# A fused layer norm, dilated attention and FFN kernel: the output product is issued ahead of the next segment's first two hidden products

## The chip, the cores and the metric

The kernel runs on one core of a Trainium2 chip. The metric is the device time of one execution in microseconds (us); lower is better. TensorE does matrix products into PSUM, ScalarE, VectorE and GpSimd work on tiles beside it, and the SyncE queue (SPq in the rows) issues the transfers. Each engine works through its own instructions in the order in which the kernel writes them, and semaphores tie the engines together.

## The reference

```python
x = L0_attn_x                                  # (16, 1024, 256), float32
xn = _layernorm(x, axis=-1)
x = x + _L0_attn_ref(xn, Wqkv, Wout) + _L0_ffn_ref(xn, W1, b1, W2, b2)

# attention: 16 heads of 16, segments of 512 tokens, every 8th token a key
scores = jnp.einsum('bhspd,bhskd->bhspk', q4, k4)          # 512 x 64 a head
scores = scores.reshape(B, H, S, nb, BLOCK_M, Kn)
c = jnp.max(scores, axis=4, keepdims=True)
w = jnp.exp(scores - c)
den = jnp.sum(w, axis=-1) + 1e-10
num = jnp.einsum('bhsnmk,bhskd->bhsnmd', w, v4)
out = num / den[..., None]                                  # then times Wout
# FFN, inner width 1024
h = jax.nn.relu(jnp.einsum('bsh,hi->bsi', hidden_states, W1) + b1)
return jnp.einsum('bsi,ih->bsh', h, W2) + b2
```

## The kernel before

The 16 x 1024 tokens are 32 segments of 512. One `step(s, ...)` handles three segments at once, each engine with a `step` of its own: the FFN and the attention's output of segment `s`, the scores, exponentials and weighted values of segment `s + 1`, and the layer norm, keys and queries of segment `s + 2`; GpSimd and VectorE prepare the statistics of `s + 3`. `first_step` and `lead_step` fill this pipeline (`s` = -2 and -1), steps 0 and 1 are written out, steps 2 to 27 run in a loop of two steps a turn, and steps 28 to 31 are written out again. The order of the work is the order of the code; no scheduler moves anything.

Every product is done in three matmuls, each operand being split into a high and a low part (`xt_hi`, `xt_lo`; `w_hi`, `w_lo`): `three_products`, line 994. The matmuls are 128 x 128 by 128 x 512. A segment's FFN has eight hidden tiles `i`: `first_product` (6 matmuls) fills `h_bank[i % 2]`, ScalarE's `hidden` makes `h_hi` (L603) and `h_full` (L605) of it, GpSimd's `hidden_lo` the difference `h_lo` (L524), and `second_product` (6 matmuls) adds tile `i` to the two y_banks. The first two hidden tiles of the next segment are made at the end of a step (`tail_tiles`); tile 2 needs the bank of tile 0 back (`h_ready`).

The attention's way through a step's end: `queries` (12 matmuls), which ScalarE casts to `q_hi` (L646); behind them on ScalarE `attention_hi` (L616, `att_hi`), and on GpSimd `attention_out` (L531) and `attention_lo` (L536, `att_lo`), the low part of the normalised attention of segment `s`. `output_product` (12 matmuls) multiplies both parts by Wout and adds them to the y_banks, which VectorE then transposes (L941). It begins with

```python
pe.wait_ge(att_hi, (s + 1) * QUADS)
pe.wait_ge(att_lo, (s + 1) * QUADS)
```

`weighted_values` (L1159) writes numerators and sums of segment `s + 1` into two pairs of banks, misc and s_banks. ScalarE's `attention_drain` copies each pair to `num_den` (L623): the first releases misc, the second s_banks, and the next step's first `scores` (L1063) wait for both, and for the packed keys `k_pack`. Both copies also release the transfer of the sums on the SyncE queue (`den_to_dram`, L381), from which VectorE makes the inverse denominators (`invert_den`, L833).

GpSimd's `inverse_deviation` (L514, L516) makes `rstd` of segment `s + 3` for the layer norm.

Of the kernel before, what the change touches and what calls it, by code (L numbers as in the profile page):

```python
# [48 lines left out]
def ln_attention_ffn(nc, x, wq_t, wkv_t, wout_t, w1, b1, w2, b2, out):  # L49
# [19 lines left out]
    with ExitStack() as ctx:  # L69
# [220 lines left out]
        def tail_tiles(s, attention):  # L290

            if isinstance(s, int) and s < 0:
                return 0, [(0, 1), (EARLY, EARLY + 1)][s + 2]
            return s + 1, (0, 1) if attention else ()
# [205 lines left out]
        def _(pool):  # L500
# [7 lines left out]
            def inverse_deviation(s, par):  # L508

                pool.wait_ge(stats_ready, s + 1)  # L510
                pool.wait_ge(xn_ready, past(s))
                pool.wait_ge(consts_made, 3)
                w = tiles(par)
                pool.tensor_tensor(var_eps[:, 0:w], mean_var[:, 0:w, 1], eps[:, 0:w], ALU.add).then_inc(var_ready, 1)  # L514
                pool.wait_ge(var_ready, s + 1)
                pool.tensor_tensor(rstd[:, 0:w], var_eps[:, 0:w], minus_half[:, 0:w],  # L516
                                   ALU.pow).then_inc(rstd_ready, 1)
# [15 lines left out]
            def attention_lo(s, quad, par):  # L533
                pool.wait_ge(att_ready, s * QUADS + quad + 1)
                pool.wait_ge(att_hi, s * QUADS + quad + 1)
                pool.tensor_tensor(att_part[1][:, quad], att[:, quad], f32(att_part[0][:, quad]),  # L536
                                   ALU.subtract).then_inc(att_lo, 1)
# [9 lines left out]
            def step(s, par, ffn, attention, norm, load):  # L547
                first, _ = tile_steps(s, ffn)
                for i in range(LAG, NH):
                    if i in first:  # L550
                        hidden_lo(past(s), first[i])
                    if i == 2 and ffn and later(s):
                        residual(s - 1, 1 - par)
                    if i == 5 and by_rows(s):
                        residual(s, par)
                if attention and ffn:
                    for quad in range(QUADS):
                        attention_out(s, quad)
                    for quad in range(QUADS):
                        attention_lo(s, quad, par)  # L560
                segment, tail = tail_tiles(s, attention)
                for i in tail:
                    hidden_lo(segment, i)
                if load:
                    inverse_deviation(s + 3, 1 - par)

            def first_step():
                inverse_deviation(0, 0)
# [22 lines left out]
        def _(act):  # L591
# [26 lines left out]
            def attention_drain(s, quad):  # L618

                n = (s + 1) * QUADS + quad + 1  # L620
                act.wait_ge(pv_psum, n)
                act.wait_ge(att_ready, past(n - QUADS))
                act.copy(num_den[:, quad], pv_banks[quad][:]).then_inc(num_den_ready, 1)  # L623
# [66 lines left out]
            def step(s, par, ffn, attention, norm, load):  # L690
                first, _ = tile_steps(s, ffn)
                for i in range(LAG, NH - 1):
                    if i == 3 and norm and par == 0:
                        keys_hi(s)
                    if attention:
                        exponential(s, i - LAG)
                    if i in first:
                        hidden(past(s), first[i])
                if ffn and not attention:
                    for quad in range(QUADS):  # L700
                        attention_hi(s, quad, par)
                if norm:
                    transposed_hi(s, par)
                if NH - 1 in first:
                    hidden(s, NH - 1)
                if attention:
                    exponential(s, PAIRS - 3)
                if attention:
                    exponential(s, PAIRS - 2)
                if norm:  # L710


                    pair_keys_hi(s, par)
                if attention:
                    exponential(s, PAIRS - 1)
                if norm:
                    for m in range(DH):
                        queries_hi(s, m)
                if attention and ffn:
                    for quad in range(QUADS):  # L720
                        attention_hi(s, quad, par)
                if attention:
                    attention_drain(s, 0)
                segment, tail = tail_tiles(s, attention)
                for i in tail:
                    hidden(segment, i)
                if attention:
                    attention_drain(s, 1)

            iterations(act, first_step, lead_step, step)  # L730

# [257 lines left out]
        def _(pe):  # L989
# [173 lines left out]
            def step(s, par, ffn, attention, norm, load):  # L1163
                first, second = tile_steps(s, ffn)
                if attention:
                    scores(s, 0)
                    scores(s, 1)
                for i in range(LAG, NH):
                    if i == 3 and norm and par == 0:
                        transpose_keys(s)  # L1170
                    if i == 5 and norm and par == 0:
                        keys_values(s)
                    if i == 6 and norm and par == 0:
                        transpose_k(s)
                    if i == NH - 1 and norm and by_tensor(s):
                        transpose_x(s, par)
                    if i in first:
                        first_product(past(s), first[i], par if ffn else 1 - par)
                    if attention and i > LAG:
                        scores(s, i - 1)  # L1180
                    if i in second:
                        second_product(past(s), second[i])
                if ffn:
                    second_product(s, NH - 2)
                if attention:
                    scores(s, NH - 1)
                if norm:
                    for m in range(DH):
                        queries(s, par, m)
                if ffn:  # L1190
                    second_product(s, NH - 1, (0,))
                if attention:
                    weighted_values_waits(s, par, norm)
                if ffn:
                    second_product(s, NH - 1, (1,))
                if attention:
                    weighted_values(s, 0, par)
                    weighted_values(s, 1, par)
                segment, tail = tail_tiles(s, attention)
                for i in tail:  # L1200
                    first_product(segment, i, 1 - par if attention else par, norm)
                if ffn:
                    output_product(s, par)

            pe.wait_ge(consts_made, 3)
            pe.wait_ge(masks_made, 2)
# [60 lines left out]
```

## Time and profile before

| | us |
|---|---|
| time, median of 3 runs | 1082.38 (1081.92 to 1085.41) |
| the profiled execution's own time | 1080.21 |
| its span in the trace | 1078.4 |
| TensorE busy | 1047.4 (97%) |
| VectorE busy | 818.8 (76%) |
| ScalarE busy | 647.9 (60%) |
| GpSimd busy | 622.7 (58%) |

Busy is the time in which an engine has an instruction in work, and all engines run side by side. The mean granted clock of TensorE is 0.997 of full speed. The ends of matmuls are modelled: a row of 0.39 us overlaps the next, and the distance between two starts is the pace.

### The profile page before, as it was taken

The page shows a single profiled execution, that of the slowest core. Times are in us where ns is not written, and L with a number is a line of the kernel's source. Part 1 is how long each engine was busy: PE and PEld are TensorE (multiplying, and loading weights), DVE is VectorE, ACT ScalarE, POOL GpSimd, SP SyncE. Part 2 cuts the span into 40 slices and gives each one's busy share as a digit, 9 for nine tenths or more (in the row PEclk, how much of TensorE's full clock was granted, in tenths as well). Part 3 has the DMA queues.
Part 4 walks back from the last instruction along what each step waited for, and adds up shares of the span by engine and source line. Part 5 has one row for each costly group of instructions (what it writes and reads, how often), then busy time and mean ns, then how long its engine had stood idle before and what let it go on. Part 6 is the DMA issues. An engine that isn't in the chain of part 4 may idle for free.

```text
span 1078.4 us, 19171 instructions
## 1 busy us (share of the span) xinstructions
PE 1047.4 (97%) x5381; PEld 813.1 (75%) x5381; DVE 818.8 (76%) x1464; ACT 647.9 (60%) x1080; POOL 622.7 (58%) x487
## 2 busy tenths in 40 slices
PE   5899999999999999999999999999999999999996
PEld 4577787777787777787777787777787777777775
DVE  7787877877877877877877777877877877878632
ACT  5656665666666566665656656566665666655651
POOL 5255565656565665565655655665565656556562
PEclk9999999999999999999999999999999999999999
DMA  5357777787877777777687887777777787866733
GB/s 190 97 154 206 221 210 212 191 233 197 234 223 192 199 214 219 225 213 209 185 234 197 231 224 191 197 215 219 221 209 217 186 229 199 242 192 182 192 108 117
DMA packets 153287, 216.37 MB, mean 201 GB/s; under 512 B 27312, under 2 KB 96432, under 8 KB 153264
## 3 DMA queue, kind: packets, MB, share of 16 engines
q1 hardware_dynamic: 153264, 216.09, 72.3%
q8 instruction: 12, 0.20, 0.1%
q14 instruction: 11, 0.09, 0.0%
HBM read 100.41 MB, written 58.46 MB: 147 GB/s over the span
## 4 chain that ended last, share of the span: by engine, by line
PE 86%; DMA 6%; DVE 3%; SPq 3%; issue 2%; ACT 1%; POOL 0%; POOLq 0%; DVEq 0%; ACTq 0%
PE h_bank L994 36%; PE y_bank L994 36%; PE s_banks L1063 5%; PE misc L1159 3%; PE s_banks L1159 2%; PE misc L994 2%; DMA k_dram<-k_lo 2%; DMA yt_dram<-y_mem 1%; SPq L399 1%; DVE xn L805 1%; DMA xt_dram<-z 1%; DMA k_pack<-k_dram 1%; SPq L438 1%; DVE s_max L822 0%; SPq L421 0%
## 5 line engine op out<-in xcount | busy, mean ns | idle before, releaser
L524 POOL TENSOR_TENSOR h_lo<-h_full,h_hi 128x512 fp32r<-128x512 f32 x256 | 335.8, 1312 | 394.0 <-ACT h_full L605 384.0
L611 ACT ACTIVATE w_exp<-w_exp 128x512 f32<-128x512 f32 x256 | 161.5, 632 | 245.8 <-DVE w_exp L828 243.9
L603 ACT ACTIVATE h_hi<-h_bank,b_cols 128x512 fp32r<-128x512 f32 x256 | 174.5, 682 | 71.2 <-PE h_bank L994 63.9
L994 PE MATMUL h_bank<-xt_hi,w_hi 128*128 128x512 f32 x512 | 206.9, 404 | 0.0
L994 PE MATMUL h_bank<-xt_lo,w_hi 128*128 128x512 f32 x512 | 200.7, 392 | 0.0
L994 PE MATMUL h_bank<-xt_hi,w_lo 128*128 128x512 f32 x512 | 200.2, 391 | 0.0
L994 PE MATMUL y_bank<-h_hi,w_hi 128*128 128x512 f32 x496 | 194.9, 393 | 1.6 <-ACT w_exp L611 1.6
L822 DVE TENSOR_REDUCE s_max<-s_banks 128x8 f32<-128x512 f32 x254 | 170.9, 673 | 33.2 <-PE s_banks L1063 33.0
L994 PE MATMUL y_bank<-h_lo,w_hi 128*128 128x512 f32 x496 | 194.0, 391 | 0.0
L994 PE MATMUL y_bank<-h_hi,w_lo 128*128 128x512 f32 x496 | 193.7, 391 | 0.0
L828 DVE TENSOR_TENSOR w_exp<-s_banks,s_max 128x512 f32<-128x512 f32 x254 | 175.7, 692 | 11.0
L605 ACT ACTIVATE h_full<-h_bank,b_cols 128x512 f32<-128x512 f32 x256 | 174.4, 681 | 0.0
L994 PEld LDWEIGHTS h_bank<-xt_hi,w_hi 128*128 128x128 f32 x512 | 96.2, 188 | 47.2 <-issue 27.1
L994 PEld LDWEIGHTS h_bank<-xt_hi,w_lo 128*128 128x128 f32 x512 | 96.4, 188 | 21.0
L994 PEld LDWEIGHTS y_bank<-h_hi,w_hi 128*128 128x128 f32 x496 | 93.6, 189 | 22.2 <-issue 2.0
L994 PEld LDWEIGHTS h_bank<-xt_lo,w_hi 128*128 128x128 f32 x512 | 96.6, 189 | 17.9
L994 PEld LDWEIGHTS y_bank<-h_lo,w_hi 128*128 128x128 f32 x496 | 93.7, 189 | 20.5
L994 PEld LDWEIGHTS y_bank<-h_hi,w_lo 128*128 128x128 f32 x496 | 93.2, 188 | 20.6
L941 DVE STREAM_TRANSPOSE y_mem<-y_bank 128x512 f32<-128x512 f32 x62 | 44.4, 717 | 77.8 <-PE y_bank L994 77.8
L1063 PE MATMUL s_banks<-q_pack,k_pack 96*128 96x512 f32 x248 | 95.2, 404 | 3.3 <-DMA k_pack<-k_dram 1.6
L536 POOL TENSOR_TENSOR att_lo<-att,att_hi 128x512 fp32r<-128x512 f32 x62 | 78.7, 1290 | 23.8 <-ACT att_hi L616 23.7
L531 POOL TENSOR_TENSOR att<-num_den,rden_rows 128x512 f32<-128x512 f32 x62 | 84.3, 1382 | 5.3 <-DMA rden_rows<-rden_dram 4.8
(135 smaller groups left out, 1513.5 us busy)
## 6 DMA issues: line engine op xcount, KB each, us to landing
q_pack<-q_hi SPq DMA_DIRECT2D x248, 128.0 KB, 2.5
x_raw<-x SPq DMA_DIRECT2D x32, 512.0 KB, 4.8
rden_rows<-rden_dram SPq DMA_DIRECT2D x128, 128.0 KB, 4.6
x_b<-x SPq DMA_DIRECT2D x32, 512.0 KB, 4.5
q_pack<-q_lo SPq DMA_DIRECT2D x124, 128.0 KB, 2.4
yt_dram<-y_mem SPq DMA_DIRECT2D x124, 128.0 KB, 3.6
y_mem<-yt_dram SPq DMA_DIRECT2D x31, 512.0 KB, 4.6
out<-x_b SPq DMA_DIRECT2D x31, 512.0 KB, 3.1
```

The lines of the kernel that those rows point to most:

```text
L524: pool.tensor_tensor(h_part[1][:, i % HBUF], h_full[:, i % HBUF], f32(h_part[0][:, i % HBUF]), ALU.subtract).then_inc(h_lo, 1)
L531: pool.tensor_tensor(att[:, quad], num_den[:, quad, 0], rden_rows[:, quad], ALU.mult).then_inc(att_ready, 1)
L536: pool.tensor_tensor(att_part[1][:, quad], att[:, quad], f32(att_part[0][:, quad]), ALU.subtract).then_inc(att_lo, 1)
L603: act.activation(h_part[0][:, i % HBUF], h_bank[i % 2][:], ACT.Relu, bias=b1_cols[:, i:i + 1]).then_inc(h_hi, 1)
L605: act.activation(h_full[:, i % HBUF], h_bank[i % 2][:], ACT.Relu, bias=b1_cols[:, i:i + 1]).then_inc(h_ready, 1)
L611: act.activation(w_exp[:, pair], w_exp[:, pair], ACT.Exp).then_inc(w_ready, 1)
L822: dve.tensor_reduce(s_max[:, pair], ps.rearrange("p t n i -> p n t i"), AX.XY, ALU.max).then_inc(max_ready, 1)
L828: dve.tensor_tensor(w_exp[:, pair].rearrange("p (t n i) -> p t n i", t=T, n=NB), ps, top, ALU.subtract).then_inc(s_shifted, 1)
L941: dve.transpose(y_blocks[:, :, a].rearrange("p i t n -> p t i n"), y_bank[a][:].rearrange("p (t i n) -> p t i n", t=T, n=PW)).then_inc(y_r ...
L994: mm = pe.matmul(ps, stationary[a], moving[b], start=start and c == 0 and n == 0, stop=stop and c == len(pairs) - 1 and n == 2, skip_group ...
L1063: pe.matmul(s_bank[n % 2], k_pack[0:PR, pair % (PAIRS // 2), pair // (PAIRS // 2)], q_pack[0:PR, pair], start=True, stop=True).then_inc(s_ ...
L1159: mm = pe.matmul(pv_banks[quad][PW * j:PW * (j + 1), a], v[rows, 1 - par, pair], w_exp[rows, pair], start=True, stop=True)
```

## The change

Three pieces of code trade places, each inside the same step and on its own engine; no instruction is added or removed. TensorE issues `output_product` of segment `s` straight behind the weighted values, and the next segment's first two hidden products behind it. ScalarE makes the second copy of the sums straight behind the first, ahead of the two hidden tiles. GpSimd makes the inverse deviations ahead of its two `h_lo`.

```diff
--- before.py
+++ after.py
@@ -558,11 +558,11 @@
                         attention_out(s, quad)
                     for quad in range(QUADS):
                         attention_lo(s, quad, par)
+                if load:
+                    inverse_deviation(s + 3, 1 - par)
                 segment, tail = tail_tiles(s, attention)
                 for i in tail:
                     hidden_lo(segment, i)
-                if load:
-                    inverse_deviation(s + 3, 1 - par)
 
             def first_step():
                 inverse_deviation(0, 0)
@@ -721,11 +721,11 @@
                         attention_hi(s, quad, par)
                 if attention:
                     attention_drain(s, 0)
+                if attention:
+                    attention_drain(s, 1)
                 segment, tail = tail_tiles(s, attention)
                 for i in tail:
                     hidden(segment, i)
-                if attention:
-                    attention_drain(s, 1)
 
             iterations(act, first_step, lead_step, step)
 
@@ -1196,11 +1196,11 @@
                 if attention:
                     weighted_values(s, 0, par)
                     weighted_values(s, 1, par)
+                if ffn:
+                    output_product(s, par)
                 segment, tail = tail_tiles(s, attention)
                 for i in tail:
                     first_product(segment, i, 1 - par if attention else par, norm)
-                if ffn:
-                    output_product(s, par)
 
             pe.wait_ge(consts_made, 3)
             pe.wait_ge(masks_made, 2)
```

TensorE, at the end of an even step in the loop, before. The rows are instructions with their waits; the first two are the weighted values, `h_bank` the first products of tiles 0 and 1, `y_bank<-att` the output product.

```order
L1159 MATMUL misc<-w_exp,v 32x512 x8
L1159 MATMUL s_banks<-w_exp,v 32x512 x8
L1005 REGISTER_ALU
L994 MATMUL h_bank0<-xt_hi,w1_hi 128x512 [waits q_lo]
L994 MATMUL h_bank0<-xt_lo,w1_hi 128x512
...
L994 MATMUL h_bank1<-xt_hi,w1_hi 128x512 [waits q_lo]
...
L994 MATMUL y_bank0<-att_hi,wout_hi 128x512 [waits att_lo,att_hi]
L994 MATMUL y_bank0<-att_lo,wout_hi 128x512
...
L1062 REGISTER_ALU [waits k_packed,num_den_ready,pair_packed0]
```

The same place after the change.

```order
L1159 MATMUL misc<-w_exp,v 32x512 x8
L1159 MATMUL s_banks<-w_exp,v 32x512 x8
L994 MATMUL y_bank0<-att_hi,wout_hi 128x512 [waits att_lo,att_hi]
L994 MATMUL y_bank0<-att_lo,wout_hi 128x512
...
L994 MATMUL h_bank0<-xt_hi,w1_hi 128x512 [waits q_lo]
L994 MATMUL h_bank0<-xt_lo,w1_hi 128x512
...
L994 MATMUL h_bank1<-xt_hi,w1_hi 128x512 [waits q_lo]
...
L1062 REGISTER_ALU [waits k_packed,num_den_ready,pair_packed0]
L1063 MATMUL s_banks<-q_pack,k_pack 128x512 [waits s_shifted] x2
L994 MATMUL h_bank0<-xt_hi,w1_hi 128x512 [waits h_ready]
```

The instruction that waits for `att_lo` and `att_hi` now stands directly behind the weighted values, and twelve first products stand between it and the scores.

ScalarE, the end of the same step, as a difference: the two copies to `num_den` and the hidden tiles.

```order
 L623 COPY num_den<-misc 128x1024 [waits att_ready]
+L621 REGISTER_ALU
+L623 COPY num_den<-s_banks 128x1024 [waits att_ready,pv_psum]
 L601 REGISTER_ALU [waits h_psum]
 L603 ACTIVATE h_hi<-h_bank0,b1_cols 128x512 [waits h_used,h_lo]
...
 L603 ACTIVATE h_hi<-h_bank1,b1_cols 128x512 [waits h_used,h_lo]
 L605 ACTIVATE h_full<-h_bank1,b1_cols 128x512
-L621 REGISTER_ALU
-L623 COPY num_den<-s_banks 128x1024 [waits att_ready,pv_psum]
```

The copy of `s_banks` moved from behind the two tiles to ahead of them.

## Rows read from the trace of the kernel before

**Rows 1.** The page, TensorE's busy time in us, share, instructions.

```profile
PE 1047.4 (97%) x5381; PEld 813.1 (75%) x5381; DVE 818.8 (76%) x1464; ACT 647.9 (60%) x1080; POOL 622.7 (58%) x487
```

**Rows 2.** TensorE's waits: us in total, times, longest us.

```profile
PE y_bank L994 <- POOL h_lo L524: 7.2, 2, 5.2
...
PE s_banks L1063 <- DMA k_pack<-k_dram: 1.6, 3, 1.0
```

**Rows 3.** Timeline of TensorE, segment 14's step: start us, us, instruction.

```profile
516.36 0.39 PE L994 MATMUL h_bank<-xt_hi,wq_lo 128*128 128x512 f32 x1
...
519.92 0.50 PE L994 MATMUL h_bank<-xt_hi,w_hi 128*128 128x512 f32 x1
...
522.77 0.39 PE L994 MATMUL y_bank<-att_hi,wout_hi 128*128 128x512 f32 x1
...
525.49 0.70 PE L1063 MATMUL s_banks<-q_pack,k_pack 96*128 96x512 f32 x2
...
527.41 0.39 PE L994 MATMUL y_bank<-h_hi,w_hi 128*128 128x512 f32 x1
```

**Rows 4.** Timelines of ScalarE, GpSimd and VectorE, the same step.

```profile
516.79 0.59 ACT L646 CAST q_hi<-h_bank 128x512 fp32r<-128x512 f32 x1
517.27 1.14 ACT L616 CAST att_hi<-att 128x512 fp32r<-128x512 f32 x2
519.31 1.01 ACT L623 COPY num_den<-misc 128x1024 f32<-128x1024 f32 x1 [0.90 <-PE misc L1159]
...
522.33 0.68 ACT L605 ACTIVATE h_full<-h_bank,b_cols 128x512 f32<-128x512 f32 x1
...
524.25 1.02 ACT L623 COPY num_den<-s_banks 128x1024 f32<-128x1024 f32 x1
...
518.03 2.53 POOL L536 TENSOR_TENSOR att_lo<-att,att_hi 128x512 fp32r<-128x512 f32 x2 [0.75 <-ACT att_hi L616]
523.16 2.65 POOL L524 TENSOR_TENSOR h_lo<-h_full,h_hi 128x512 fp32r<-128x512 f32 x2 [2.59 <-ACT h_full L605]
...
526.05 1.02 POOL L516 TENSOR_TENSOR rstd<-var_eps,minus_half 128x4 f32<-128x4 f32 x1
...
520.93 0.38 DVE L760 BATCH_NORM_AGGREGATE mean_var<-stats 128x2 f32<-128x6 f32 x4
```

**Rows 5.** Timelines of GpSimd and TensorE, last segment.

```profile
1063.54 1.71 POOL L524 TENSOR_TENSOR h_lo<-h_full,h_hi 128x512 fp32r<-128x512 f32 x1
...
1065.39 0.55 PE L994 MATMUL y_bank<-w_hi,h_hi 128*128 128x256 f32 x1 [5.17 <-POOL h_lo L524]
```

**Rows 6.** Timelines of GpSimd and TensorE, steps of segments 0 and 29.

```profile
64.84 2.54 POOL L536 TENSOR_TENSOR att_lo<-att,att_hi 128x512 fp32r<-128x512 f32 x2 [3.73 <-ACT att_hi L616]
...
66.17 0.50 PE L994 MATMUL h_bank<-xt_hi,w_hi 128*128 128x512 f32 x1
...
1005.53 2.53 POOL L536 TENSOR_TENSOR att_lo<-att,att_hi 128x512 fp32r<-128x512 f32 x2 [0.52 <-ACT att_hi L616]
...
1007.15 0.50 PE L994 MATMUL h_bank<-xt_hi,w_hi 128*128 128x512 f32 x1
```

**Rows 7.** Timeline of ScalarE, segment 30's step.

```profile
1036.90 1.01 ACT L623 COPY num_den<-misc 128x1024 f32<-128x1024 f32 x1 [1.17 <-PE misc L1159]
...
1041.81 1.02 ACT L623 COPY num_den<-s_banks 128x1024 f32<-128x1024 f32 x1
```

**Rows 8.** The chain that ended last: start us, us, what held it.

```profile
1043.48 1.88 DMA den_dram<-num_den
...
1070.30 4.56 PE y_bank L994 x36
```

**Rows 9.** Windows: stretch, length, busy us (count) by engine, granted clock, DMA share, GB/s.

```profile
44.00:48.00 4.00, 0.84 (x4) 0.58 (x5) 3.53 (x5) 0.84 (x2) 1.19 (x1) 1.00 0.83 204
48.00:51.40 3.40, 3.40 (x10) 2.62 (x9) 3.33 (x9) 1.01 (x3) 0.00 (x0) 0.50 0.82 178
...
104.00:108.00 4.00, 3.25 (x14) 2.69 (x15) 2.36 (x5) 0.14 (x1) 1.66 (x3) 1.00 0.69 146
```

## The prediction

> **What bounds the kernel now.** I began with the busy shares: TensorE is busy for 97% of the span [rows 1]. Next I read what TensorE itself waits for [rows 2]. Its waits on GpSimd sum to 7.2 us in two places, both in the last segment, and its waits on the packed keys to 1.6 us in three places. Nothing else of the 32 segments' steady work shows in that list, so TensorE is the bound and has almost no idle time that an order could give back. A change of order can then do three things: open a hole in TensorE's row, close one of the few that exist, or move the two ends of the program.
>
> Then I read one step of the loop around the change, first on TensorE [rows 3]. The last query product starts at 516.36, behind the weighted values the first product of the next segment's tile 0 at 519.92, the output product at 522.77, and the next step's scores at 525.49. Each block of 12 matmuls takes 2.72 us (522.77 to 525.49), that is 0.227 us a matmul; the first block takes 2.85 because its first weight load is not hidden.
>
> The other engines' rows of the same step [rows 4] give what the output product needs. ScalarE casts the second half of the queries from 516.79 (the last query matmul ends at 516.36 + 0.39 = 516.75), then casts att_hi from 517.27. GpSimd starts att_lo at 518.03, behind the first of these casts, and makes both quads in 2.53 us: it is done at **520.56**. So att_lo comes 3.8 us behind TensorE's own last query matmul, whatever else the step does. Before, the output product starts 2.2 us later than that, and never waits.
>
> **The output product, moved ahead of the two first products.** It now wants to start where the first product started, at 519.92. It waits for both quads of att_lo, which end 0.64 us later. From GpSimd's end to TensorE's start I take the one place that shows it, in the last segment [rows 5]: h_lo ends at 1063.54 + 1.71 = 1065.25, the matmul starts at 1065.39, so 0.14. The output product starts at 520.70, and the stall is 520.70 - 519.92 = **0.78 us** a step. TensorE's sequence is fixed, so all that is queued behind the waiting matmul (12 output matmuls, 12 first products, the scores) moves by this much; nothing fills the hole. The weight load that is exposed behind a wait was exposed at this place before too, so it adds nothing.
>
> Does the stall stay in every step? The step shown is segment 14's. Its two rows, att_lo's end and the start of the matmul behind the weighted values, stand 0.64 to 0.66 us apart in each of the 28 steps from segment 1 to 28, since both hang on TensorE's query products; 28 x 0.78 = 21.8. Two steps lie outside that pattern [rows 6]: segment 0, att_lo ends 67.38 against 66.17, stall 1.21 + 0.14 = 1.35; segment 29, 1008.06 against 1007.15, 0.91 + 0.14 = 1.05. Segment 30 is part of the end, below. Together **24.2 us**.
>
> **The first products, 2.72 us later.** Tile 0's chain is now closer to its users. In the step shown its first matmul starts at 519.92, ScalarE's h_full ends at 523.01 and GpSimd's h_lo starts at 523.16 [rows 3, 4]. Less the 0.1 us of exposed load that the new place does not have, h_full ends 2.99 and h_lo of tile 0 about 3.14 + 1.3 = 4.44 us behind the first matmul. TensorE needs h_full after 12 matmuls (2.72) and two scores, and h_lo after six matmuls more. Scores and six matmuls take 527.41 - 525.49 = 1.92, of it the six 1.38, so the needs come at 3.26 and 4.64. With 0.14 for the signal they are there at 3.13 and 4.58. Both just fit, by 0.13 and 0.06, where before they had seconds. A weight load cannot then run far ahead, so a little may show: at least nothing, at most 0.15 us at each of two places (an exposed load costs 0.1). I take 0.05 us a step over 30 steps, **1.5 us**; the bounds are 0 and 9.
>
> **The copy of the second sums ahead of the tiles (ScalarE).** In the step shown it moves from 524.25 to right behind the first copy, 519.31 + 1.01 = 520.3 [rows 4]. ScalarE is idle there until tile 0 arrives, and that now arrives later, so it costs nothing. Before, it ended at 525.27, 0.22 us ahead of the scores that wait for it: just in time, and hidden. So in the loop the earlier copy gives nothing. It lets the queue send the denominators some 1.5 us earlier, in the shadow of 97% TensorE; no gain.
>
> **The inverse deviations ahead of the tiles (GpSimd).** Their statistics end at 520.93 + 0.38 = 521.31 [rows 4], and they take 0.2 and 1.02 us (the second is the rstd row), in a stretch where GpSimd now waits for tile 0's h_full until 520.70 + 2.82 + 2.99 = 526.5. Hidden. If that cover were gone, 1.2 us would fall on h_lo and, at a slack of 0.06, nearly all on TensorE; the statistics would have to be 4 us later for that.
>
> **Waits that the stall absorbs.** TensorE's three waits for the packed keys, 1.03 at the most, 1.6 in all [rows 2], stand at the scores. The keys' chain hangs on the query products, so a TensorE that arrives 0.8 us later waits for 0.25 at one place and not at the other two: **-1.3 us**.
>
> **The end.** Here the copy does pay. In segment 30's step no later work hides it: the chain that ended last runs from this copy of the sums over the denominators' transfer to the last matmuls at 1070.30 [rows 8]. In that step the first copy starts at 1036.90 and the second at 1041.81 [rows 7]. Behind the first it would start at about 1036.90 + 0.96 = 1037.86: 3.95 us earlier. TensorE's row near the end has 5.17 us of waiting [rows 5], more than those 3.95 plus the step's own stall (1.35 in the worst step above), so the whole chain moves up and segment 30's stall disappears in it: **-3.95 us**.
>
> **Sum.** 24.2 + 1.5 - 1.3 - 3.95 = +20.4 us. The profiled execution took 1080.21 us (span 1078.4 and 1.8 around it), which gives 1100.6. The median shown is 2.2 us above that execution, which gives 1102.8. Between the two I predict **1102**.
>
> **Rivals.**
> (a) *No stall, only the end's gain.* The output product finds att_lo ready, and the end's 3.95 us (with up to 1.5 lost at tile 0) makes it 1082.4 - 3.95 = **1078 to 1080, faster**. It decides at 0.78 us: ScalarE's casts or GpSimd's two subtractions would have to end that much earlier against the query products. Against it: the change moves nothing that stands ahead of them on either engine, and the distance is constant over 28 steps. For it: only the inferred ends of matmuls and of GpSimd's instructions, which this reading trusts to some tenths. 8%.
> (b) *Part of the stall, about 3.95 / 28 = 0.14 us a step*, so that loss and gain cancel, within 0.3% of 1082: 3%.
> (c) *A second stall behind the first.* Tile 0's chain, with 0.06 us of slack, misses by more than the signal's time, for example because the wait is held in TensorE's instruction queue ahead of the matmul and the next loads start cold: 0.2 to 0.4 us more a step, x 30 = 6 to 12 us on top, **1107 to 1113**. 9%.
> (d) *The clock.* Behind 44 to 48 us, in which TensorE was busy for 0.84 us, the stretch from 48 to 51.4 has a granted clock of 0.50, the lower level of 1.2 GHz [rows 9]; at half the pace it loses 1.7 us. If each stall did that, 30 x 1.7 = 51 us would come on top, **1153**. Against it: the stretch from 104 to 108 us, which holds the wait of 1.03 us for the keys, longer than the stall foreseen, has a granted clock of 1.00 [rows 9]. 2%. The Trainium skill speaks for this rival: "TensorE: Matmul & The Clock Gate", section "A second HAM failure mode: psum-queue depth-cycling", says that frequent short idle times between groups of matmuls can make the clock swing between its two levels. By that rule the time would be (d)'s; the trace, with one such wait and no fall, does not bear it out, though it shows none that recurs.
>
> **How the numbers follow.** My forecast of one stall a step holds 78%. Its own range is 1096 (the exposed load behind the wait hidden, 28 x 0.1 less, no cost at tile 0, and the profiled run's base) to 1107. The 80% range adds part of (c), at its bound of 9 us at tile 0: **1096 to 1110**. What measures as no change here is 0.3%, about 3 us. Faster by more is (a), 8%; within it (b), 3%; slower everything else, 89%.
>
> **What the new profile would show.** TensorE idle 0.6 to 0.8 us before y_bank<-att_hi in every step, released by GpSimd's att_lo, some 20 us in the list of waits in 28 to 31 places. The second num_den copy right behind the first, and the rstd rows ahead of the h_lo rows. Nearly no wait for k_pack. Step pairs of the loop longer by 1.6 us. From the second copy of the last attention step to the end, the same 36 to 37 us as before. The prediction is wrong if the output product starts within 0.2 us of the weighted values' end; if the waits stand at h_bank or y_bank<-h_hi instead (c); if the granted clock leaves 1.0 inside the loop (d); or if the end does not come 4 us closer to segment 30's weighted values.

## The result, and the profile after

| | before | after |
|---|---|---|
| median, us | 1082.15 (1081.91 to 1085.41, 4 runs) | 1101.86 (1099.53 to 1104.19, 4 runs) |
| profiled execution, us | 1080.21 | 1099.53 |
| span, us | 1078.4 | 1097.7 |

The change makes the kernel slower: ratio 1.018, 95% interval [1.015, 1.0209]. The forecast was 1102, range 1096 to 1110.

The first lines of the page after, with the span and the busy times. TensorE has 4.3 us more of busy time than in [rows 1], though it does the same matmuls; the span has 19.3 us more. So most of the loss must be waiting.

```profile
span 1097.7 us, 19171 instructions
PE 1051.7 (96%) x5381; PEld 813.3 (74%) x5381; DVE 819.5 (75%) x1464; ACT 653.1 (59%) x1080; POOL 640.0 (58%) x487
```

TensorE's waits after (us in total, times, longest). Against [rows 2] one group is new, 30 waits on att_lo; h_lo is down from 7.2 us in two places to 3.2 in one; the row for k_pack is gone. The 1.2 us put down to "issue" is the output product of segment 0.

```profile
PE y_bank L994 <- POOL att_lo L536: 21.6, 30, 0.9
...
PE y_bank L994 <- POOL h_lo L524: 3.2, 1, 3.2
...
PE y_bank L994 <- issue: 1.2, 1, 1.2
```

TensorE's timeline of the same step as in [rows 3] (segment 14's). The output product starts at 532.11, 1.78 us behind the row of the weighted values, where a start without a wait came at 1.00 (518.92 to 519.92 before). The difference is the stall: 0.78. The last two rows show a second, small effect: h_bank's last matmul to the first y_bank is 0.31 instead of 0.23, and the next distance is 0.33.

```profile
530.33 1.06 PE L1159 MATMUL s_banks<-w_exp,v 64*32 64x512 f32 x16
532.11 0.47 PE L994 MATMUL y_bank<-att_hi,wout_hi 128*128 128x512 f32 x1 [0.72 <-POOL att_lo L536]
...
534.95 0.39 PE L994 MATMUL h_bank<-xt_hi,w_hi 128*128 128x512 f32 x1
...
537.67 0.63 PE L1063 MATMUL s_banks<-q_pack,k_pack 96*128 96x512 f32 x2
...
539.29 0.39 PE L994 MATMUL h_bank<-xt_hi,w_lo 128*128 128x512 f32 x1
539.60 0.49 PE L994 MATMUL y_bank<-h_hi,w_hi 128*128 128x512 f32 x1
539.93 0.40 PE L994 MATMUL y_bank<-h_lo,w_hi 128*128 128x512 f32 x1
```

ScalarE and GpSimd in that step, the answer to [rows 4]. att_lo ends at 529.44 + 2.53 = 531.97, and TensorE starts 0.14 later. The two copies stand side by side; the rstd rows stand ahead of h_lo, in idle time.

```profile
530.71 1.01 ACT L623 COPY num_den<-misc 128x1024 f32<-128x1024 f32 x1 [0.90 <-PE misc L1159]
531.62 1.02 ACT L623 COPY num_den<-s_banks 128x1024 f32<-128x1024 f32 x1
...
529.44 2.53 POOL L536 TENSOR_TENSOR att_lo<-att,att_hi 128x512 fp32r<-128x512 f32 x2 [0.74 <-ACT att_hi L616]
...
533.43 1.34 POOL L516 TENSOR_TENSOR rstd<-var_eps,minus_half 128x4 f32<-128x4 f32 x1
538.07 2.66 POOL L524 TENSOR_TENSOR h_lo<-h_full,h_hi 128x512 fp32r<-128x512 f32 x2 [3.30 <-ACT h_full L605]
```

Where the 19.3 us of span lie, in us between starts of the weighted values' row on s_banks (each start read from the timelines). These stretches come back below for the experiments.

| | start to step 3 | 24 loop steps, 3 to 27 | steps 27 to 30 | step 30 to the end | span |
|---|---|---|---|---|---|
| before | 162.84 | 776.46 | 97.28 | 41.82 | 1078.4 |
| after | 163.89 | 797.44 | 97.54 | 38.83 | 1097.7 |
| difference | +1.05 | +20.98 | +0.26 | -2.99 | +19.3 |

The end. ScalarE's last two copies, in segment 30's step: the second now starts 0.91 us behind the first, where [rows 7] had 4.91.

```profile
1059.19 1.01 ACT L623 COPY num_den<-misc 128x1024 f32<-128x1024 f32 x1 [1.17 <-PE misc L1159]
1060.10 1.02 ACT L623 COPY num_den<-s_banks 128x1024 f32<-128x1024 f32 x1
```

The chain that ended last (start, us) still begins with that copy and ends in the same 36 matmuls. But these took 6.05 us, where [rows 8] have 4.56.

```profile
1061.77 1.88 DMA den_dram<-num_den
...
1088.13 6.05 PE y_bank L994 x36
```

The windows show the clock at that place. First after (columns: stretch, length, busy us and count for PE, PEld, DVE, ACT and POOL, granted clock, share of DMA, GB/s), then before:

```profile
1088.00:1091.00 3.00, 2.87 (x15) 2.90 (x16) 0.00 (x0) 0.00 (x0) 0.00 (x0) 0.60 0.02 5
1091.00:1095.00 4.00, 3.17 (x23) 2.96 (x21) 1.38 (x2) 0.00 (x0) 0.00 (x0) 0.87 0.15 56
```

```profile
1070.00:1076.00 6.00, 4.54 (x36) 4.37 (x36) 1.38 (x2) 0.00 (x0) 0.15 (x1) 1.00 0.13 46
```

After, the last product begins behind an idle time of 3.2 us and runs at a granted clock of 0.60, near the lower level of 1.2 GHz. Before, a low clock came too, but earlier, behind the wait of 5.17 us [rows 5], where TensorE had little to do (columns: stretch, length, PE busy, clock, share of DMA, GB/s):

```profile
1062.00:1066.00 4.00, 0.61 (x3) 0.89 0.01 4
1066.00:1070.00 4.00, 2.29 (x11) 0.68 0.33 131
```

### The profile page after: what moved, and what is told of

Same layout as the page of the kernel before. It is cut to its first block and busy times, and to the rows that moved or that the text cites. A ratio compares the mean times of both kernels' runs of the same rounds, so it can differ in the third digit from the quotient of the medians.

```text
span 1097.7 us, 19171 instructions
## 1 busy us (share of the span) xinstructions
PE 1051.7 (96%) x5381; PEld 813.3 (74%) x5381; DVE 819.5 (75%) x1464; ACT 653.1 (59%) x1080; POOL 640.0 (58%) x487
## 5 line engine op out<-in xcount | busy, mean ns | idle before, releaser
L822 DVE TENSOR_REDUCE s_max<-s_banks 128x8 f32<-128x512 f32 x254 | 171.8, 677 | 116.2 <-PE s_banks L1063 115.9
L994 PE MATMUL h_bank<-xt_hi,w_hi 128*128 128x512 f32 x512 | 203.1, 397 | 0.0
L994 PE MATMUL y_bank<-h_hi,w_hi 128*128 128x512 f32 x496 | 197.6, 398 | 1.6 <-ACT w_exp L611 1.6
L828 DVE TENSOR_TENSOR w_exp<-s_banks,s_max 128x512 f32<-128x512 f32 x254 | 175.6, 691 | 11.0
L994 PEld LDWEIGHTS h_bank<-xt_hi,w_lo 128*128 128x128 f32 x512 | 96.4, 188 | 20.4
L861 DVE TENSOR_TENSOR xt_lo<-xt_raw,xt_hi 128x512 fp32r<-128x512 f32 x58 | 37.5, 688 | 59.8 <-ACT xt_hi L642 59.8
```

The source lines that it names most:

```text
L822: dve.tensor_reduce(s_max[:, pair], ps.rearrange("p t n i -> p n t i"), AX.XY, ALU.max).then_inc(max_ready, 1)
L828: dve.tensor_tensor(w_exp[:, pair].rearrange("p (t n i) -> p t n i", t=T, n=NB), ps, top, ALU.subtract).then_inc(s_shifted, 1)
L861: dve.tensor_tensor(token_order(xt[1][:, par, c]), block_order(xt_raw[:, c]), token_order(f32(xt[0][:, par, c])), ALU.subtract).then_inc(x ...
L994: mm = pe.matmul(ps, stationary[a], moving[b], start=start and c == 0 and n == 0, stop=stop and c == len(pairs) - 1 and n == 2, skip_group ...
```

## The experiments

The theory to test was the prediction's: TensorE waits for att_lo, 0.78 us a step, and the other two parts matter at the end alone. The rival: the order as such costs time (tile 0's chain, the clock), so that a product placed elsewhere would not get the 20 us back. The comparisons with the kernel before were made on other chips than the result's, where its median was 1084.05 to 1085.10; each ratio is against runs on the same chip. 

**copy_only**: the kernel before with ScalarE's part alone.

```diff
                 if attention:
                     attention_drain(s, 0)
+                if attention:
+                    attention_drain(s, 1)
                 segment, tail = tail_tiles(s, attention)
                 for i in tail:
                     hidden(segment, i)
-                if attention:
-                    attention_drain(s, 1)
```

> The kernel before with only ScalarE's second copy of the sums moved ahead of the two hidden tiles. Theory A (in the loop the change costs what TensorE waits for att_lo, and the copy pays only at the end): nothing changes in the loop, the steps keep 64.56 us a pair; the end comes 3.95 us closer, of which up to 1.5 us may be lost to a lower granted clock in the last 36 matmuls: 1078.2 to 1079.7 us. Rival B (the copy is what costs in the loop, by holding up ScalarE ahead of tile 0): tile 0's h_hi starts later and the time is 1082 or more.

Measured: 1076.99 us (6 runs) against 1085.10, ratio 0.9932 [0.991, 0.9954]. That is more than the end alone. By the trace (span 1074.5) the stretches are -0.15, -1.69, -0.02 and -2.04 us against before's: part of the gain lies in the loop. Rows of SyncE's queue, the transfer of the sums and the keys of the following step, show what moved there; first before, then copy_only:

```profile
525.30 1.17 SPq L381 DMA_DIRECT2D den_dram<-num_den  x2
...
547.27 0.43 SPq L354 DMA_DIRECT2D k_dram<-k_hi  x1
...
553.12 1.28 SPq L364 DMA_DIRECT2D k_pack<-k_dram  x3
```

```profile
523.65 1.17 SPq L381 DMA_DIRECT2D den_dram<-num_den  x2
...
546.42 0.32 SPq L354 DMA_DIRECT2D k_dram<-k_hi  x1
...
551.50 1.44 SPq L364 DMA_DIRECT2D k_pack<-k_dram  x3
```

The queue waits at `den_to_dram` for the second copy; with the copy early it sends the sums, the keys and the packed keys 1.65, 0.85 and 1.62 us earlier (of which 0.1 to 0.15 is the whole step's earlier place). Why the packed keys gain more than the keys was not followed. TensorE's waits for the keys fall from 1.6 us [rows 2] to 0.6. The profiled executions lie 3.9 us apart and the medians 8.1: before's runs on that chip spread over 6.5 us, and before's trace is of a quick execution (1080.21 us). What such a quick one does not show of before stands under deviation_only.

**queue_late**: copy_only, but SyncE sends the sums no sooner than the next step's first scores are done. ScalarE's copy stays early, so that only the queue is late.

```diff
-            def den_to_dram(s):
+            def den_to_dram(s, held=False):
 
-                sp.wait_ge(num_den_ready, (s + 1) * QUADS)
+                if held:
+                    sp.wait_ge(s_psum, (s + 1) * PAIRS + 1)
+                else:
+                    sp.wait_ge(num_den_ready, (s + 1) * QUADS)
...
-                    den_to_dram(s + 1)
+                    den_to_dram(s + 1, norm)
```

> copy_only, but the SyncE queue sends the denominators of a segment only when the first scores of the next step are done, some 0.6 us later than in the kernel before (not in the last two steps, where the queue has nothing behind it). Theory Q (the early copy also helps in the loop, because the queue, held until 525.3 by the copy's end, runs 1.6 us late, and brings the packed keys late to the scores): the waits for k_pack come back, and of the 8 us that copy_only gained the 4 us of the loop are lost: 1080 to 1084 us on a chip where before takes 1082 to 1085. Rival E (all of the gain is at the end, the rest is chance between runs): as copy_only, 1076 to 1079 us.

Measured: 1086.74 us (12 runs) against 1084.05, ratio 1.0031 [1.0013, 1.0048], above the range of either theory but on theory Q's side. The gain in the loop is lost and more (24 steps in 782.85 us, copy_only 774.77, before 776.46), while the end keeps its part (38.79 us against before's 41.82). TensorE's list of waits names the keys ten times:

```profile
PE s_banks L1066 <- DMA k_pack<-k_dram: 6.5, 10, 1.3
```

So a late queue does cost time in the loop, through the packed keys: it is all that differs from copy_only. The experiment holds the queue longer than before did, so that it shows the way of the copy's effect and not its size.

**deviation_only**: the kernel before with GpSimd's part alone (`inverse_deviation` ahead of the two `hidden_lo`).

> The kernel before with only GpSimd's part. Theory A: no difference, within 0.3% of before; TensorE's waits for the packed keys and the one of 1.6 us behind the loop stay, since neither its code nor the SyncE queue moves. Rival C: 3 us or more away from before.

Measured: 1083.58 us (12 runs) against 1084.05, ratio 0.999 [0.997, 1.001]. Nothing in the time, in the order of before. Its profiled execution took 1084.15 us, near the medians of before on these chips, and its trace (span 1082.4) shows where a usual execution is slower than the quick one behind before's trace: +3.07, +0.40, -1.14 and +1.67 us in the four stretches. In the first, TensorE's wait for the keys ahead of the loop is 1.97 us instead of 1.03, and the clock falls behind it; in the last, the final product takes 5.99 us instead of 4.56, at the low clock, though the copy stands where before has it (columns as in the windows above, TensorE alone):

```profile
106.00:110.00 4.00, 3.76 (x10) 0.58 0.70 147
...
1072.00:1076.00 4.00, 3.18 (x15) 0.50 0.01 4
```

Against this trace copy_only's stretches are -3.22, -2.09, +1.12 and -3.71 us, together -7.9: the size of its gain in the medians. That such executions are the usual ones of before is an inference from their times; only one was traced.

**product_only**: the kernel before with TensorE's part alone (`output_product` ahead of the two `first_product`).

> The kernel before with only TensorE's part of the change: output product behind the weighted values, the first two products behind it. Theory A: besides the 0.78 us at att_lo, ScalarE's second copy of the sums now stands behind two tiles that come 3.5 us later, and the next scores wait for it: it would end about 28.75 us into a step in which TensorE is ready at 26.25 (counted as in the step shown, 520 added), so 2.7 us more a step, 80 us in all, and 3.4 us at the end: 1180 to 1195 us, with TensorE's waits at s_banks released by ScalarE's num_den. Rival B (the copy's place in the loop does not matter to TensorE): 1100 to 1106 us.

Measured: 1207.82 us (2 runs), ratio 1.1153 [1.1122, 1.1183]: slower than the expected 1180 to 1195 by another 13 to 28 us. The stall on att_lo is the same as in after; what is new stands at the next scores. TensorE's waits, then one of them:

```profile
PE s_banks L1063 <- issue: 42.3, 17, 2.5
PE s_banks L1063 <- ACT num_den L623: 32.0, 13, 2.5
PE y_bank L994 <- POOL att_lo L536: 21.4, 30, 0.7
```

```profile
623.57 0.72 PE L1063 MATMUL s_banks<-q_pack,k_pack 96*128 96x512 f32 x2 [2.47 <-ACT num_den L623]
```

The second copy, left behind both hidden tiles on ScalarE, comes as much later as the tiles do, and 30 scores wait up to 2.5 us each. 13 of the waits are put down to num_den by name; the other 17 end 0.1 to 0.2 us behind the same copy. The copy's move is part of what makes the product's move affordable.

What the expectation left out is the clock. Behind these waits it falls in some steps and stays in others: in 15 of the 30 steps matmuls behind the scores start 0.43 us apart instead of 0.23. Two places, each from the wait on; the first falls and the second does not:

```profile
513.00:519.00 6.00, 6.00 (x15) 0.50 0.58 143
...
550.40:556.00 5.60, 5.59 (x25) 1.00 0.48 116
```

The 24 loop steps take 877.6 us, twelve of the quickest pairs (71.56) would take 858.7: 19 us in the loop, the size of the excess. The mean granted clock is 0.969. This is the prediction's rival (d), at 2.5 us of waiting and not at 0.7.

**product_and_copy**: after without GpSimd's part, that is with `inverse_deviation` behind the two `hidden_lo` as before.

```diff
-                if load:
-                    inverse_deviation(s + 3, 1 - par)
                 segment, tail = tail_tiles(s, attention)
                 for i in tail:
                     hidden_lo(segment, i)
+                if load:
+                    inverse_deviation(s + 3, 1 - par)
```

> The changed kernel without GpSimd's part (the inverse deviations stay behind the two h_lo). Theory A: they are off the path in either place: the same as the changed kernel, 1099 to 1104 us. Rival C (they matter where tile 0 has no slack, through VectorE, which waits for rstd ahead of the scores' maxima): 3 us or more away from it.

Measured: 1170.7 us (4 runs), ratio 1.0813 [1.0791, 1.0836], 69 us above after. My own theory (A) falls, the rival that this part carries something holds. GpSimd's and VectorE's rows in one of the steps:

```profile
606.51 2.66 POOL L524 TENSOR_TENSOR h_lo<-h_full,h_hi 128x512 fp32r<-128x512 f32 x2 [6.10 <-ACT h_full L605]
...
609.40 1.18 POOL L516 TENSOR_TENSOR rstd<-var_eps,minus_half 128x5 f32<-128x5 f32 x1
```

```profile
610.85 0.41 DVE L772 TENSOR_SCALAR xn_keys<-x_keys,mean_var,rstd 128x256 f32<-128x256 f32 x1 [5.67 <-POOL rstd L516]
```

GpSimd stands idle for 6.1 us waiting for a hidden tile that the change made late, with the short rstd instructions queued behind it. VectorE waits 5.67 us for them, and behind `xn_keys` in its queue stand the softmax rows of the same step (L822, L828). TensorE then waits for these and for xn_keys:

```profile
PE s_banks L1063 <- DVE w_exp L828: 23.6, 16, 1.5
...
PE misc L1108 <- DVE xn_keys L772: 19.5, 15, 2.4
```

With 5.4 us for the keys these groups hold 45 us more of waiting than after's list, and TensorE's busy time is 19 us longer. What lengthens the busy time was not followed.

**dose**: after, with two more GpSimd subtractions of 128 x 128 ahead of each step's att_lo, whose results nobody uses. If att_lo's end sets TensorE's start, the stall grows by their duration.

```diff
...
+                if quad == 0:
+                    for half in range(2):
+                        pool.wait_ge(dose_made, past(s * 2 + half))
+                        pool.tensor_tensor(k_mask_t[:], att[:, quad, half * P:(half + 1) * P],
+                                           f32(att_part[0][:, quad, half * P:(half + 1) * P]),
+                                           ALU.subtract).then_inc(dose_made, 1)
                 pool.tensor_tensor(att_part[1][:, quad], att[:, quad], f32(att_part[0][:, quad]),
                                    ALU.subtract).then_inc(att_lo, 1)
```

> The changed kernel with more of the suspected wait: two further GpSimd subtractions of 128x128 ahead of att_lo in each step, their results not used. From the rows of before (0.2 us for 128x4, 1.27 for 128x512) I estimate 0.47 each, 0.94 us a step. Theory A: every us by which att_lo is later is a us of TensorE, 30 x 0.94 = 28 us more than the changed kernel, 1130 us (1120 to 1140); the exact number is 30 times the duration that its trace shows. Rival B: at most 5 us more, below 1107.

Measured: 1130.65 us (4 runs), ratio 1.042 [1.0391, 1.0449]. One step, GpSimd and then TensorE: two added instructions that put off att_lo's row by 0.96 us (577.88 to 578.84), and a wait of 1.66 instead of 0.72, that is +0.94. Over 30 steps that makes 28 us; after itself was not timed on this chip, but its median of 1101.86 and the 1100.62 of changed_again, below, lie 29 and 30 us lower.

```profile
577.88 1.01 POOL L540 TENSOR_TENSOR k_mask_t<-att,att_hi 128x128 f32<-128x128 f32 x2 [0.73 <-POOL att L532]
578.84 2.51 POOL L543 TENSOR_TENSOR att_lo<-att,att_hi 128x512 fp32r<-128x512 f32 x2
```

```profile
581.50 0.47 PE L1001 MATMUL y_bank<-att_hi,wout_hi 128*128 128x512 f32 x1 [1.66 <-POOL att_lo L543]
```

The clock, in windows with TensorE alone (stretch, length, busy, granted clock, share of DMA, GB/s). The step just shown keeps 1.00; segment 0's, with its wait of 2.1 us at 67 to 70, does not.

```profile
67.00:70.00 3.00, 1.24 (x4) 0.85 0.84 205
70.00:73.00 3.00, 3.00 (x10) 0.58 0.73 180
580.00:584.00 4.00, 2.50 (x11) 1.00 0.85 221
584.00:588.00 4.00, 4.00 (x19) 1.00 0.71 147
```

**high_part_first**: after, but the output product does its eight matmuls with att_hi first and waits for att_lo only ahead of the last four (the last segment keeps its order). The computation is the same but for the order of its additions.

```diff
                 pe.wait_ge(att_hi, (s + 1) * QUADS)
-                pe.wait_ge(att_lo, (s + 1) * QUADS)
...
+                    for b in range(YB):
+                        for m in range(DH):
+                            for n in range(2):
+                                pe.matmul(y_bank[b][:], wout[n][:, m, b * P:(b + 1) * P], att_part[0][:, m],
+                                          start=False, stop=False, skip_group_check=True)
+                    pe.wait_ge(att_lo, (s + 1) * QUADS)
+                    for b in range(YB):
+                        for m in range(DH):
+                            mm = pe.matmul(y_bank[b][:], wout[0][:, m, b * P:(b + 1) * P], att_part[1][:, m],
+                                           start=False, stop=m == DH - 1, skip_group_check=True)
```

> The changed kernel, its output product in another order: the 8 matmuls with att_hi first, behind a wait for att_hi alone, then the wait for att_lo and its 4 matmuls. Theory A: att_lo is needed 8 x 0.227 = 1.8 us later and is there by then, so the 30 waits (24.2 us by their size) are gone and nothing else changes: 1101.9 - 24.2 = 1077.7, plus 0.16 us a step that tile 0's short cover costs (it stays, 28 x 0.16 = 4.5), so 1078 to 1083 us. Rival B (the place of the product or the clock costs, not the wait for att_lo): 1095 us or more.

Measured: 1076.88 us (6 runs), ratio 0.9925 [0.9902, 0.9949]. TensorE's list of waits has no att_lo any more. With all three parts in the order of after, taking the wait away turns a loss of 1.8% into a gain of 0.75%: the order as such costs little.

**between** and **between_again** (the same kernel, timed a second time on another chip): after, but the output product stands between the two first products, where the six matmuls of tile 0, some 1.4 us, cover att_lo's 0.64.

```diff
+                segment, tail = tail_tiles(s, attention)
+                for i in tail[:1]:
+                    first_product(segment, i, 1 - par if attention else par, norm)
                 if ffn:
                     output_product(s, par)
-                segment, tail = tail_tiles(s, attention)
-                for i in tail:
+                for i in tail[1:]:
                     first_product(segment, i, 1 - par if attention else par, norm)
```

> The changed kernel, but with the output product between the two first products (tile 0, output product, tile 1). Theory A: the product starts 6 matmuls later than in the changed kernel, 0.7 us behind att_lo's end, and never waits; tile 0 keeps its old lead: the loop takes 64.5 us a pair as before, the end keeps its gain: 1078 to 1080 us. Rival B (any output product ahead of a first product costs): between 1085 and 1095 us.

> The version with the output product between the two first products, once more beside the one above: 1072 to 1076 us, and within 1.5 us of it if the copy is the whole gain.

Measured: 1074.14 us (6 runs), ratio 0.99 [0.9877, 0.9923], and 1073.27 us (6 runs), ratio 0.989 [0.9868, 0.9913]: faster than both kernels, and the best version of the study. Of the 30 waits for att_lo one of 0.3 us is left in the first trace and none in the second.

**copy_and_deviation** (the two other parts in TensorE's order of before) and **changed_again** (the changed kernel once more) went with it.

> The kernel before with ScalarE's and GpSimd's parts, TensorE's order untouched. If TensorE's new place brings nothing by itself even where it does not wait, this equals copy_only and the version with the product between the tiles: 1074 to 1078 us. If the place between the tiles helps by itself, it is 2 us or more slower than that one in the same session.

> The changed kernel once more, on a chip and in a session where before is timed too: 1099 to 1104 us, 27 us above the version between the tiles: 30 waits (24.2 us) and 0.17 us a step for tile 0's late h_lo (28 x 0.17 = 4.8), less 2 us or so of chance at the ends.

Measured on the same chip: copy_and_deviation 1077.26 us, ratio 0.9932 [0.9909, 0.9955]; changed_again 1100.62 us, 1.0146 [1.012, 1.0172]. The changed kernel lies 27.35 us above between_again, as expected; between_again lies 4.0 us below copy_and_deviation, over the 2 us that the expectation named as the sign that this place helps by itself. The stretches of the traces:

| | 24 loop steps | steps 27 to 30 | step 30 to the end | span |
|---|---|---|---|---|
| copy_and_deviation | 775.19 | 96.17 | 39.36 | 1073.7 |
| between | 774.40 | 95.12 | 38.89 | 1072.1 |
| between_again | 774.40 | 95.08 | 38.23 | 1071.3 |
| high_part_first | 778.79 | 95.11 | 38.55 | 1075.2 |
| changed_again | 797.19 | 97.43 | 38.83 | 1099.6 |
| product_and_copy | 851.56 | 106.08 | 37.44 | 1168.0 |

Between's loop is 0.8 us shorter (copy_and_deviation still has 1.3 us of waits for the keys, between_again none), its steps behind the loop by 1.1, and its end by 0.5 and 1.1; the span, whose start is longer, by 1.6 and 2.4. So this place for the output product gains a little over before's, and most of the gain over the kernel before is the two other parts'.

## Why the prediction was right, and where its steps were not

**The stall: right.** 28 steps show +1.78 us behind the weighted values instead of +1.00; the rows of segments 0 and 29 stand at 2.27 and 1.93, which is 1.27 and 0.93 where 1.35 and 1.05 were said. Sum 28 x 0.785 + 1.27 + 0.93 = 24.2 us, as predicted. That GpSimd's end sets the start is shown twice: dose lengthens the wait by what it puts ahead of att_lo, high_part_first and between take it away.

**Tile 0: mechanism right, size off.** The term was 0.05 us a step. h_lo of tile 0 ended 4.45 us behind the first matmul (538.07 + 1.33 - 534.95), as said. But TensorE needed it after 4.57 and not 4.64 (539.29 + 0.23 - 534.95): scores and six matmuls take 1.85 us here, while the 1.92 of [rows 3] had some exposed load in the scores. With 0.14 for the signal h_lo is 0.02 late instead of 0.06 early; the wait shows as 0.08 and exposes the next load, 0.10 more. That is 0.18 in this step. On average it is 0.16: two undisturbed steps take 64.56 us before and 66.45 after, +1.89, of it 1.57 for two stalls. The trace has it in 25 steps and not in 30 (the wait and the exposed load are missing in the first ones and in those behind the loop), so the term is about 4.0 us instead of 1.5. It lies inside the bounds of 0 to 9. High_part_first, which has no stall, still takes 64.89 a pair.

**The keys' waits: -1.3 said, about -2.7 found.** The row is gone. In the loop before, 24 steps took 776.46 us, 1.7 more than twelve undisturbed pairs of 64.56; after, 797.44 is twelve pairs of 66.45, with nothing over. Ahead of the loop, at the wait of 1.03 us, the scores start 0.47 us behind the last matmul where before had 1.42: 0.24 of the wait is left, the 0.25 that the prediction said. The rows name the keys for only 0.6 of the loop's 1.7, so that the rest of it is counted here without proof. TensorE comes later, as reckoned, but copy_only shows that the keys also come earlier.

**"So in the loop the earlier copy gives nothing": wrong.** Copy_only's loop is 1.7 us shorter than before's. The sentence looked for the copy's user on TensorE alone. Its other user is the in-order SyncE queue, which held the keys' transfers behind the sums (copy_only, queue_late). And with the product moved, the copy in its old place costs some 2.5 us at each scores (product_only): its value depends on the part beside it.

**The deviations: "hidden" right, "nearly all" of 1.2 us as the price of lost cover never tried.** Moved ahead they cost nothing (deviation_only), and they close the wait of 1.59 us told below. What the step missed most is the other direction: had they stayed behind the tiles, the kernel would have lost 69 us (product_and_copy), because VectorE needs them and would wait for a tile that has nothing to do with them. Costing each part against the kernel before could not show it.

**The end: -3.95 said, -2.99 found.** ScalarE's second copy ends 2.25 us behind the weighted values' row (1060.10 + 1.02 - 1058.87), where it ended 6.25 behind (1041.81 + 1.02 - 1036.58): -4.0, as foreseen. The chain loses 1.49 of it in the last 36 matmuls, at the low clock, and wins back some 0.5 on its way. By the prediction's own sign ("if the end does not come 4 us closer") this term failed against before's trace. Its other sign misread the rows: from the second copy to the end before has 35.6 us (1078.4 - 1042.83), not 36 to 37; after has 36.6. But the 1.49 cannot be laid to the change. Deviation_only, with the copy in its old place, has the last product at 5.99 us; product_and_copy, with the copy early, has 4.56; of the 13 traces only this one and before's have 4.56, all others 5.95 to 6.98. Against deviation_only's end of 43.49 us after's is 4.7 shorter. What decides in which matmuls the low clock falls is open.

**Rival (d), the clock: rightly refused for this change.** In the loop 30 waits of 0.7 us left the clock at 1.00, and the mean is 0.997 as before. Its mechanism exists in this program all the same, at waits of 2.5 us (product_only).

**Not foreseen: a wait of 1.59 us that the profile puts down to nothing**, in before, in the first step behind the loop. It is gone in after. Rows of VectorE and TensorE:

```profile
947.81 0.41 DVE L772 TENSOR_SCALAR xn_keys<-x_keys,mean_var,rstd 128x256 f32<-128x256 f32 x1 [1.02 <-POOL rstd L516]
...
956.56 0.38 DVE L778 TENSOR_TENSOR xkey_lo<-misc,xkey_hi 128x256 fp32r<-128x256 f32 x1
```

```profile
957.05 0.47 PE L994 MATMUL misc<-wkv_hi,xkey_hi 128*128 128x512 f32 x1 [1.59 <-issue]
```

The code makes this matmul wait for `xkey_lo`, which VectorE ends at 956.94, 0.11 us earlier, and VectorE was late because it had waited 1.02 us for the rstd row. So it is GpSimd's part that closes the wait. Copy_only and queue_late, without that part, have the same 1.57 and 1.59 us, product_and_copy 2.3; every one of them starts 0.10 us behind xkey_lo's end. Of the traces with GpSimd's part only copy_and_deviation shows such a wait, of 0.45 us. Product_only, without the part, has none of that length: its matmul too starts 0.11 us behind xkey_lo's end, but TensorE itself comes late there. Why VectorE's row is the last to come in this step alone, and what the 1.59 hold beyond the 1.02, was not followed.

The sum as found, against the span: stalls 24.2, tile 0 about 4.0 (0.16 in 25 steps), the keys -2.7, the end -3.0, the wait behind the loop -1.6, and the first weighted values 0.5 earlier (37.97 instead of 38.52) give +20.4 for the 19.3 measured. The remaining 1.1 us lie in no row that I can name, half of it ahead of step 3 and half behind the loop; the loop's +20.98 comes out to 0.1. The prediction's +20.4 came nearer than its parts deserved: tile 0 was too small and the end too large, and the two gains that it undercounted or missed made up for both. And 19.3 is the distance of two single traces, before's a quick one: changed_again lies 16.1 us above before's median on its own chip.

## What to carry to other kernels

Before moving a consumer ahead in TensorE's queue, set the end of its producer against the start of what it overtakes: 0.64 us late in each of 28 steps is the whole result, and the six matmuls of tile 0 put back between the two take all of it off again. Cost the parts of a change in pairs as well as alone, since a copy worth 8 us and a 1.2 us instruction worth nothing in the old order were worth tens of us in the new one, by standing behind something that had become late. And read more than one trace of the kernel before: a quick execution hid a longer wait, and a low clock in the last product, that deviation_only's trace, of the same time in the median, has.

## What the runs showed of the hardware

- The clock: waits of 0.72 us (after) and 1.66 us (dose) that come back in every step left the granted clock at 1.00 in the loop; waits of 2.3 to 2.5 us that come back in every step (product_only) were followed by the low clock in 15 of 30 steps; single waits of 2.0 us (deviation_only, ahead of the loop), 2.1 us (dose, segment 0) and 3.2 us (after, the end) were followed by stretches of 0.58, 0.58 and 0.60. The Trainium skill, "TensorE: Matmul & The Clock Gate", section "A second HAM failure mode: psum-queue depth-cycling", says that short idle times between groups of matmuls can swing the clock between its levels. Product_only's trace agrees with it at 2.5 us; after's and dose's show none of it at 0.72 and 1.66.
- From the end of GpSimd's row to the start of the TensorE matmul that waits for it, the traces have 0.14 us (531.97 to 532.11, and 1065.25 to 1065.39 in before).
- A wait that the profile puts down to "issue" can have a releaser: the 1.59 us in before end 0.11 behind VectorE's xkey_lo, 17 waits in product_only 0.1 to 0.2 behind ScalarE's copy.
